# The last tile's front sums inside the preceding tile's step, its weighing directly after, and the last store issued from two queues

## The reference

```python
# conditioning: grouped convolution, 9 taps, 4 groups, plus a linear map of cond and a bias
out = conv1d(x, weight, padding=4, groups=4) + (c @ c_weight.T)[:, :, None] + bias[None, :, None]
# ffn over rows of 512
base_out = out @ base_W.T + base_b
probs    = softmax(out @ router_W.T + router_b)        # 15 routes
topk_p, topk_i = top_k(probs, 8)
w        = sum of topk_p by expert_map[topk_i]         # one weight for each of 8 experts
h        = out @ A.T                                   # 8 experts x rank 16 = 128 columns
lora     = (h * w) @ B * 2.0
return x + base_out + lora
```

## Time and profile before

| | us |
|---|---|
| median of 3 runs | 201.48 |
| lowest, highest | 200.59, 201.67 |
| the profiled execution | 201.99 |
| its span, first to last instruction | 200.2 |

### The profile page before, as it was taken

The page is one execution under the profiler, slowest core; times in us unless marked ns, Lnnn a source line. Parts: engine busy times, 40 slices in busy tenths (PEclk is TensorE's granted clock), DMA queues, the critical chain, the costliest instruction groups (busy, mean ns, idle before and its releaser), DMA issues.

```text
span 200.2 us, 4334 instructions
## 1 busy us (share of the span) xinstructions
PE 190.6 (95%) x1304; PEld 182.0 (91%) x1304; DVE 163.1 (82%) x548; ACT 76.5 (38%) x196; POOL 143.1 (72%) x113
## 2 busy tenths in 40 slices
PE   7798699999999999999999999999999999998993
PEld 2667499999999999999999999999999999997992
DVE  1399898888888889898888888888998889775662
ACT  5164253344444343334444443433344444122210
POOL 5359988777777778887777777788777777852520
PEclk9999879999999999999999999999999999999999
DMA  6994044334445444434443444444334223333312
GB/s 163 296 393 146 21 138 143 128 114 147 119 149 165 158 158 155 145 121 129 138 139 122 158 158 158 158 140 147 124 122 154 67 90 108 105 105 110 105 52 105
DMA packets 18955, 27.78 MB, mean 139 GB/s; under 512 B 2112, under 2 KB 10176, under 8 KB 18944
## 3 DMA queue, kind: packets, MB, share of 16 engines
q1 hardware_dynamic: 18688, 27.11, 41.2%
q0 software_dynamic: 112, 0.28, 0.8%
q10 hardware_dynamic: 144, 0.26, 0.4%
HBM read 19.25 MB, written 8.39 MB: 138 GB/s over the span
## 4 chain that ended last, share of the span: by engine, by line
PE 85%; POOL 4%; DMA 4%; DVE 3%; issue 1%; ACT 1%; SPq 1%; DVEq 0%; ACTq 0%
PE wide_ps L486 54%; PE conv_banks L469 15%; PE wide_ps L510 11%; DMA x_in<-x_start 4%; POOL is_expert L420 2%; PE conv_banks L486 2%; PE hwt_bank L497 2%; POOL terms_lo L404 1%; POOL y_lo L410 1%; DVE y_rows L588 1%; PE odd_bank L440 0%; POOL map_f L417 0%; DVE y L672 0%; PE conv_banks L510 0%; DVE xr L583 0%
## 5 line engine op out<-in xcount | busy, mean ns | idle before, releaser
L486 PE MATMUL wide_ps<-wide_hi,y_hi 128*128 128x400 f32 (+1 forms) x248 | 80.6, 329 | 1.0 <-DVE xr L583 0.9
L486 PE MATMUL wide_ps<-wide_lo,y_hi 128*128 128x400 f32 (+1 forms) x248 | 76.5, 313 | 0.5 <-DVE wide_lo L221 0.5
L486 PE MATMUL wide_ps<-wide_hi,y_lo 128*128 128x400 f32 (+1 forms) x248 | 76.5, 313 | 0.0
L404 POOL TENSOR_TENSOR terms_lo<-terms,terms_hi 128x768 fp32r<-128x768 f32 x28 | 51.7, 1847 | 30.8 <-ACT terms_hi L334 30.8
L486 PEld LDWEIGHTS wide_ps<-wide_hi,y_hi 128*128 128x128 f32 x248 | 46.6, 189 | 3.6 <-issue 1.2
L486 PEld LDWEIGHTS wide_ps<-wide_lo,y_hi 128*128 128x128 f32 x248 | 46.8, 190 | 0.8 <-DVE wide_lo L221 0.8
L486 PEld LDWEIGHTS wide_ps<-wide_hi,y_lo 128*128 128x128 f32 x248 | 46.5, 189 | 0.0
L399 POOL TENSOR_TENSOR xr<-xr,biases_sb 128x512 f32<-128x512 f32 x32 | 41.7, 1302 | 6.5 <-DMA xr<-x_rows 6.4
L410 POOL TENSOR_TENSOR y_lo<-y,y_hi 128x512 fp32r<-128x512 f32 x32 | 41.5, 1296 | 3.1 <-ACT y_hi L341 3.0
L348 ACT ACTIVATE hw_hi<-hwt_bank 128x128 fp32r<-128x128 f32 x32 | 8.9, 277 | 88.1 <-PE hwt_bank L497 88.1
L341 ACT ACTIVATE y_hi<-y 128x512 fp32r<-128x512 f32 x32 | 20.2, 632 | 17.8 <-PE wide_ps L486 17.0
(11 more groups left out here) (91 smaller groups left out, 266.5 us busy)
## 6 DMA issues: line engine op xcount, KB each, us to landing
xr<-x_rows SPq DMA_DIRECT2D x32, 256.0 KB, 2.7
out<-xr SPq DMA_DIRECT2D x31, 256.0 KB, 2.0
even<-x_even SPq DMA_DIRECT2D x28, 132.0 KB, 2.5
terms<-x_odd SPq DMA_DIRECT2D x28, 128.0 KB, 2.8
wide_sb<-wide_w SPq DMA_DIRECT2D x2, 656.0 KB, 9.0
x_in<-x_start SPq DMA_DIRECT2D x2, 260.0 KB, 5.4
x_in<-x_start SPq DMA_DIRECT2D x1, 520.0 KB, 10.6
biases_sb<-biases POOLq DMA_DIRECT2D x1, 263.5 KB, 6.8
```

Source lines behind the costliest of these rows:

```text
L404: nc.gpsimd.tensor_tensor(terms_lo[i % 2][:, :, :, :], terms[i][:, :, :, :], terms_hi[i % 2][:, :, :, :].bitcast(F32), ALU.subtract)\
L486: mm = nc.tensor.matmul(sums_of(t, k)[:, b, 0:columns[1] - columns[0]], a[k % 2][:, r, :], w[:, r, columns[0]:columns[1]], start=r == 0 an ...
```

## The change

PE: the last three steps become `last_steps`. Step 30 does the front bank of tile 30, `turn_hw(29)`, runs 0 and 1 of the next bank of 30, then the whole front bank of tile 31 (it waits for y_lo of 31 and for `add_out(28)`), `up(29)`, and runs 2 and 3 of the next bank of 30. Step 31 does `turn_hw(30)`, the next bank of 31, `turn_hw(31)`, now into `odd_bank`, and `up(30)`. Step 32 does `up(31)` alone; the four matmuls on zeros are gone.

DVE: in step 30 `add_out(29)` is left out; step 31 does `choose(31)`, `add_out(29)`, `mark(31)`, `weigh(31)`, `hw_low(30)`; step 32 does `hw_low(31)`; `add_out(30)` follows it, ahead of the halves of 31. ACT: in step 31 the exponentials of 31 go ahead of `hw_high(30)`; at its end it issues the store of the second half of tile 31. SP stores the first half alone.

```diff
--- before.py
+++ after.py
@@ -44,7 +44,7 @@
 FIRST_UNIT = START * HALVES
 UNROLL = 4
 
-WARM_UP, WARM_BETWEEN, WARM_END = 9, 7, 4
+WARM_UP, WARM_BETWEEN = 9, 7
 
 
 def build(nc, x_start, x_even, x_odd, x_rows, conv_w, cond, wide_w, up_w, biases, expert_map, out):
@@ -229,6 +229,10 @@
                 return conv_banks[:, :, :] if t == TILES - 2 else wide_ps[0][:, :, :]
             return wide_ps[k % 2][:, :, :]
 
+        def hwt_of(t):
+
+            return odd_bank[:, 0:P] if isinstance(t, int) and t == TILES - 1 else hwt_ps
+
         def linear_sums(t, k):
             flat = sums_of(t, k).rearrange("p b n -> p (b n)")
             return flat[:, FRONT:FRONT + 2 * (BANK - FRONT)]\
@@ -283,11 +287,9 @@
 
             steps_of(sync, step)
             last = (TILES - 1) % XRING
-            for b in range(2):
-                columns = slice(b * HALF, (b + 1) * HALF)
-                sync.wait_ge(out_added, TILES + b)
-                sync.dma_start(out[TILES - 1, :, columns], xr[last][:, columns])\
-                    .then_inc(stored[last], 16)
+            sync.wait_ge(out_added, TILES)
+            sync.dma_start(out[TILES - 1, :, 0:HALF], xr[last][:, 0:HALF])\
+                .then_inc(stored[last], 16)
             for i in range(XRING):
                 sync.wait_ge(stored[i], 16 * (TILES // XRING + (1 if i == last else 0)))
 
@@ -345,7 +347,7 @@
                 if from_tile(t, 2):
                     act.wait_ge(out_done, t - 1)
                 act.wait_ge(hwt_done, t + 1)
-                nc.scalar.activation(hw_hi[k % 2][:, :], hwt_ps, ACT.Copy)\
+                nc.scalar.activation(hw_hi[k % 2][:, :], hwt_of(t), ACT.Copy)\
                     .then_inc(hw_hi_ready, 1)
 
             wide_high(range(RUNS // 2))
@@ -365,6 +367,10 @@
             def step(t, k, p):
                 if from_tile(t, 1) and up_to_tile(t, TILES - 2):
                     y_high(t + 1, k + 1)
+                if isinstance(t, int) and t == TILES - 1:
+                    exponentials(t, k)
+                    hw_high(t - 1, k - 1)
+                    return
                 if from_tile(t, 1):
                     hw_high(t - 1, k - 1)
                 if up_to_tile(t, TILES - 1):
@@ -375,6 +381,10 @@
                     odd_up(t + 6, (k + 2) % URING)
 
             steps_of(act, step)
+
+            last = (TILES - 1) % XRING
+            act.wait_ge(out_added, TILES + 1)
+            act.dma_start(out[TILES - 1, :, HALF:], xr[last][:, HALF:]).then_inc(stored[last], 16)
 
         @block.gpsimd
         def _(pool):
@@ -494,7 +504,7 @@
                 if not from_tile(t, 1):
                     pe.wait_ge(ident_ready, 1)
                 pe.wait_ge(hw_ready, t + 1)
-                nc.tensor.transpose(hwt_ps, hw[k % 2][:, :], ident[:, :])\
+                nc.tensor.transpose(hwt_of(t), hw[k % 2][:, :], ident[:, :])\
                     .then_inc(hwt_done, 1)
 
             def up(t, k, groups=((FRONT_BANK, NEXT_BANK),)):
@@ -546,20 +556,39 @@
                 conv_second_pair(0)
                 conv_second_pair(1)
 
+            def last_steps(t, k):
+
+
+                if t == TILES - 2:
+
+                    pe.wait_ge(y_lo_ready, t + 1)
+                    pe.wait_ge(y_rows_ready, TILES - 2)
+                    linear(t, k, range(RUNS), (FRONT_BANK,)).then_inc(front_done, 1)
+                    turn_hw(t - 1, k - 1)
+                    linear(t, k, range(2), (NEXT_BANK,))
+                    pe.wait_ge(y_lo_ready, t + 2)
+                    pe.wait_ge(out_added, t - 1)
+                    linear(t + 1, k + 1, range(RUNS), (FRONT_BANK,)).then_inc(front_done, 1)
+                    up(t - 1, k - 1)
+                    linear(t, k, range(2, RUNS), (NEXT_BANK,)).then_inc(linear_done, 1)
+                elif t == TILES - 1:
+                    turn_hw(t - 1, k - 1)
+                    linear(t, k, range(RUNS), (NEXT_BANK,)).then_inc(linear_done, 1)
+                    turn_hw(t, k)
+                    up(t - 1, k - 1)
+                else:
+                    up(t - 1, k - 1, ((FRONT_BANK,), (NEXT_BANK,)))
+
             def step(t, k, p):
                 runs = range(RUNS)
-                if isinstance(t, int) and t == TILES:
-                    keep_warm(odd_bank[:, :], WARM_END)
-                    turn_hw(t - 1, k - 1)
-                    return up(t - 1, k - 1, ((FRONT_BANK,), (NEXT_BANK,)))
+                if isinstance(t, int) and t >= TILES - 2:
+                    return last_steps(t, k)
                 if isinstance(t, int) and t == 0:
                     first_step()
                 else:
                     pe.wait_ge(y_lo_ready, t + 1)
-                    if from_tile(t, 2) and up_to_tile(t, TILES - 3):
+                    if from_tile(t, 2):
                         pe.wait_ge(out_added, t - 1)
-                    elif t == TILES - 2:
-                        pe.wait_ge(y_rows_ready, TILES - 2)
                     linear(t, k, runs, (FRONT_BANK,)).then_inc(front_done, 1)
                     turn_hw(t - 1, k - 1)
                     linear(t, k, runs[:3], (NEXT_BANK,))
@@ -680,7 +709,7 @@
                 dve.wait_ge(hw_hi_ready, t + 1)
                 if from_tile(t, 2):
                     dve.wait_ge(out_done, t - 1)
-                nc.vector.tensor_tensor(hw_lo[k % 2][:, :], hwt_ps,
+                nc.vector.tensor_tensor(hw_lo[k % 2][:, :], hwt_of(t),
                                         hw_hi[k % 2][:, :].bitcast(F32), ALU.subtract)\
                     .then_inc(hw_lo_ready, 1)
 
@@ -733,6 +762,14 @@
                     difference(t + 5, (k + 1) % URING)
                 if up_to_tile(t, TILES - 1):
                     choose(t, k)
+                if isinstance(t, int) and t == TILES - 1:
+
+                    add_out(t - 2, (k - 2) % UNROLL)
+                    dve.wait_ge(top_ready, t + 1)
+                    mark(t, k)
+                    weigh(t, k)
+                    hw_low(t - 1, k - 1)
+                    return
                 if from_tile(t, 1):
                     hw_low(t - 1, k - 1)
                 if up_to_tile(t, TILES - 1):
@@ -740,11 +777,12 @@
                         dve.wait_ge(map_ready, 1 + E)
                     mark(t, k)
                     weigh(t, k)
-                if from_tile(t, 1) and up_to_tile(t, TILES - 1):
+                if from_tile(t, 1) and up_to_tile(t, TILES - 3):
                     add_out(t - 1, (k - 1) % UNROLL)
 
             steps_of(dve, step)
 
+            add_out(TILES - 2, (TILES - 2) % UNROLL)
             dve.wait_ge(xr_biased, TILES)
             for b in range(2):
                 half = xr[(TILES - 1) % XRING][:, b * HALF:(b + 1) * HALF]
```

## The result

| | before | after |
|---|---|---|
| median, us (22 runs each, taken together) | 201.68 | 201.07 |
| ratio after to before | | 0.9964, 95% interval 0.9948 to 0.9980 |
| span of the profiled execution | 200.2 | 199.4 |

The kernel became faster by 0.36%, about 0.7 us (the two medians differ by 0.61), against a forecast of 0.6, from 201.48 to 200.9. Two more measurements of the changed kernel gave 0.9969 (0.9947 to 0.9990) and 0.9942 (0.9919 to 0.9965).

A forecast was written before the change was run, and what follows sets the result against it. PE bounds the kernel (85% of the chain), then a relay; +1.41 PE, -0.64 and -0.17 for the adds, +0.30 zeros, +0.1 second queue, about -0.4 stores give 0.6 us: 201.48 to 200.9, range 200.1 to 201.6.

The forecast's parts named there:

- PE in step 30: Front bank of tile 31 moved up on PE: ends at 191.16, 1.41 us earlier; logits start at 191.20.
- `add_out(29)` on the path: On DVE ahead of `mark(31)`, waiting for `up(29)`: starts at 191.98, takes 0.64 of the 1.41 us; hw ends 194.15.
- The zeros: Matmuls on zeros gone ahead of the last transpose on PE: lag from hw 0.30 instead of 0.60, gain 0.30 us.
- rival B: Lag to the transpose is 0.14 (0.16 more) and the stores don't collide (0.3 more): 200.4 us, chance 0.22.
- `add_out(30)` on the path: On DVE between `hw_low(31)` and the last tile's halves: first half starts 0.17 us later behind the transpose.
- The halves' end: DVE's last two half adds end at 196.90 against 197.80, 0.90 us earlier.
- The stores: Last stores of tiles 30 and 31: contention and SP's order cost about 0.4 us; last landing 199.03 against 199.6.
- the second queue: Last half's store issued from ACT instead of SP: worth 0.1 us of issue time.
- rival C: ACT's queue lands the last half late, 2.6 us behind its issue, at 199.5: 201.4 us, chance 0.17.
- rival D: PE's clock falls in the idle time where the matmuls on zeros stood: slower, 202.5 us, chance 0.06.
- Rival E: y_lo of 31 comes over 0.6 us late and PE stands still in step 30: 201.5 us, chance 0.04.
- the wait costs nothing: PE's wait for y_lo of 31 before its front bank in step 30 is free, with 0.6 us left.

The follow-up runs named there:

- y_first_add_late: Changed kernel with POOL's y_low(31) ahead of bias_rows(30), and add_out(29) moved on DVE behind hw_low(30): ratio to before 0.9950, tail 10.79 us.
- no_zeros: Kernel before without the four matmuls on zeros, nothing else: ratio to before 0.9984 (0.9964 to 1.0005), tail 11.47 us.
- sp_only: Changed kernel with both halves of the last store issued by SP: ratio to before 0.9972, tail 11.68 us.
- no_store30: Changed kernel with the store of tile 30 left out: ratio to before 0.9947, tail 10.81 us.
- after_again: The changed kernel measured a second time, unaltered: ratio to before 0.9969, tail 12.01 us.
- y_first: Changed kernel with POOL running y_low(31) ahead of bias_rows(30) in step 30: ratio to before 0.9958, tail 11.11 us.
- after_look: The changed kernel measured a third time, unaltered: ratio to before 0.9942, tail 11.19 us.
- y_first_up_early: y_first_add_late with PE's step 31 reordered, up(30) ahead of the transpose of 31: ratio to before 0.9936, tail 10.65 us.

## Why the prediction was right, point by point

- **PE in step 30**: front of 31 with its logits at 191.24, predicted 191.20 (1.41 earlier; it measured 1.43 after taking out the 0.06 by which this execution is late). Right where the load was in time.
- **`add_out(29)` on the path**: start 192.03, predicted 191.98; hw's end 194.21, predicted 194.15; y_first_add_late shows that it was on the path. I had not said that the alternative was open and worth 0.3 (0.32 of tail).
- **The zeros**: mis-sized. I put the lag from hw to the transpose at 0.30, near its upper bound, a gain of 0.30. From hw to ACT the time fell from 0.97 to 0.48 in both after and no_zeros, so the gain was 0.49. Half of rival B, a lag at its lower bound, came true: the transpose started 194.26 - 194.21 = 0.05 behind the end of hw, under the 0.14 that I had taken as the least, though ACT then followed its start by 0.43 and not by 0.37.
- **`add_out(30)` on the path**: predicted 0.17 lost. From ACT's start to the halves it is 196.03 - 194.69 = 1.34 against 1.15, 0.19 lost.
- **The halves' end**: 8.55 behind the logits of 30 against 9.63, 1.08 earlier; predicted 0.90. The difference is the zeros.
- **The stores**: predicted about 0.3 given back (0.90 to 0.6); it measured 2.62 - 2.40 = 0.22 (0.26 by the finer ends). But the two terms inside were wrong together: 0.1 for the second queue beside a full contention can't both be true, since what the second half saves at its issue it then spends behind tile 30's data. sp_only gives the queue 0 to 0.07, no_store30 gives the contention 0.36 to 0.43. The part of rival B that the stores don't collide is refuted. On ACT's queue, rival C, nothing landed late: its half took 2.1 from issue to landing in the profile after, as the half on SP's queue did, and C needed 2.6. The landings came in the order and near the times of the prediction: tile 30 at 198.18 (198.25), the second half, last, at 198.92 (199.03); before, the last came at 199.68.
- **The clock** (rival D): 1.00 through the relay. It fell only behind the last matmul, when nothing was left.
- **Rival E was underrated**, and this is the step of the reasoning that failed: "the wait costs nothing". I had 0.6 of cover, from an execution in which POOL waited for ACT by 0.15, and I had the spread of the loads up to 4.1. What I didn't work out is that 0.15 is nearly no cover, and that POOL's wait would pass from ACT to the load in the next execution. The 0.6 itself was right: seen from the logits of 30, y_lo of 31 ended 1.42 later in after_again (188.28 - 186.99 = 1.29, against 188.04 - 188.17 = -0.13 before) and 1.06 later in sp_only, and less 0.6 that is 0.82 and 0.46, the losses measured. Two of the five executions of the table lost them, one of the three of the change itself. The cover was sized right, and how often it would be used up was not.

That the forecast came out so near the measured 0.7 has luck in it: the sum was short by 0.26 for the execution of the profile (0.86 instead of 0.6), and it left out a loss that only some executions have. These two errors have opposite signs. That the second one offset the first in the median is an argument and isn't shown, since y_first, which can't have the loss, has a ratio that doesn't differ from the change's.

## What to carry to other kernels

When a step is moved up, look at what stands ahead of its producer in that engine's queue, and take the cover from the latest of its possible releasers over many executions, not from the one that came last in one trace. When work is taken off one engine's tail, see which in-order instruction of the next engine stands between, since their orders have to change together: with PE's and ACT's changed and DVE's not, the kernel was 0.19% slower than before. The second queue for the last stores gained next to nothing here, with the DMA engines full; moving the store ahead out of their way gained 0.3 behind the last add and gave 0.2 of it back ahead of it.

## What the runs showed of the hardware

The time from the issue of one load of 256 KB to its use varied from 3.22 to 5.37 us between executions of the same code, though the DMA traffic around it was nearly over. In the windows of after_again the DMA share from 3.5 us behind the issue on was almost nothing:

```profile
183.30:183.80 0.50, 0.50 (x7) 0.50 (x6) 0.47 (x5) 0.09 (x2) 0.00 (x0) 1.00 0.16 49
183.80:184.30 0.50, 0.50 (x7) 0.50 (x6) 0.46 (x2) 0.00 (x0) 0.00 (x0) 1.00 0.00 0
```

yet POOL was released only at 185.75. A load of 256 KB is complete when 16 parts have reported, and the trace has the time of each: 15 of them came 2.52 to 3.08 behind the issue, and one alone at 5.29. In that gap lie two packets. The DMA view of 183.60 to 183.70 has this one, of an instruction queue, which started at 183.66 and took 0.94:

```profile
q8 instruction: 1, 0.02, 58.7%
```

and that of 184.55 to 184.65 has this one, of 4 bytes, the last of the load, which started at 184.58, as the other ended:

```profile
q1 hardware_dynamic: 1, 0.00, 1.6%
```

In the profile after, where the load was in time, one view of 0.1 us (184.25 to 184.35) has both, and there the 4 bytes ended at 184.30, where the instruction packet began:

```profile
q8 instruction: 1, 0.02, 58.1%
q1 hardware_dynamic: 1, 0.00, 0.6%
```

The traces of this study all have this packet near this load, and they fall in three kinds:

| the instruction packet of q8 | executions | the load's 16th part landed behind its issue |
|---|---|---|
| behind the load's last 4 bytes, or clear of them | nine | 2.7 to 3.7 |
| ahead of data of the load, which goes on when it ends | after_look, y_first_up_early | 4.2, 4.5 |
| between the data and the last 4 bytes | sp_only, after_again | 4.9, 5.3 |

In all of them the other 15 parts had landed by 3.1. So the late load is one of its 16 parts that stood behind a fetch of instructions (0.93 to 1.43 us). The trace doesn't name the DMA engine of a packet; that the two shared one is inferred from starts and ends that agree within 0.02, and why the order differs between executions stays open.

The same idle time of PE near 23 us (1.87 in before, 1.86 in y_first) was followed by a granted clock of 0.50 in one execution and of 1.00 in the other:

```profile
24.00:27.00 3.00, 3.00 (x21) 2.96 (x20) 2.57 (x12) 2.21 (x6) 1.91 (x2) 1.00 0.56 174
```

That row is of y_first. The changed kernel did both: behind 1.87 of idle the granted clock was 0.50 in after, behind 1.86 it was 1.00 in after_look. So an idle time of this length may or may not cost the clock, from one execution to the next.
